# Joins of the stages in a two-layer transformer behind a causal attention, on one core

## The chip, the cores and the metric

The kernel runs on one core of one Trainium2 chip. The metric is the device time of one execution in microseconds, median of several runs. TensorE is PE in the profile, VectorE DVE, ScalarE ACT, GpSimd POOL, SyncE SP; SPq is the queue in which SP issues its DMAs, in order.

## The reference, cut to what matters

The input is x of 16 batches x 512 rows x 128 columns. A first part normalises the rows and computes causal attention; its result is added to the result of a two-layer transformer over the same normalised rows at the end. All is in float32. Here `shift_token` gives each row the second half of the row before it; that is what the "shifted rows" below are.

```python
def shift_token(t):
    t1, t2 = jnp.split(t, 2, axis=-1)
    t2 = jnp.pad(t2, ((0, 0), (1, 0), (0, 0)))[:, :-1]
    return jnp.concatenate([t1, t2], axis=-1)

def _layer(x, wqkv, qs, ksc, wo, lg, lb, w1, b1, w2, b2):
    h = shift_token(x)
    q, k, v = jnp.split(h @ wqkv, 3, axis=-1)        # 8 heads of 64
    q = l2norm(q) * qs
    k = l2norm(k) * ksc
    q, k = rotary_xpos(q, k)
    x = x + local_attention(q, k, v) @ wo            # window 64 and the one before
    h = shift_token(x)
    h = layernorm(h) * lg + lb
    a, g = jnp.split(h @ w1 + b1, 2, axis=-1)
    return x + (a * gelu(g)) @ w2 + b2
...
```

The first part is `softmax((q k^T + causal + bias) / 64) v` over 16 heads, times Wo, plus bo.

## The kernel before

There are five pieces of work, and each is a block: a block ends when all engines have done their part of it, and only then the next begins.

- `causal_attention` (L107) works through 16 batches of 8 slots, a slot being a pair of heads. SP loads the batches and stores the results (`turn`, L234); POOL scales the probabilities (L301). The normalised rows stay in the buffer `xf`, and the results are stored to `out` batch by batch.
- A block in `transformer` (L1329; the block is L1376 to L1424) prepares the rest: SP loads the rope table, the weights of layer 0 and the shifted rows of batch 0 into `hs`, and reads the 4 MB of `out` back into `acc` (L1386). DVE clears buffers, and POOL builds the masks.
- `local_attention` (L755) goes through 64 tiles of 128 rows, one per slot, with a pipeline five slots deep (`tile_slots`, L687; slot (b, t) is tile t of batch b, and (16, 0) is the last of the slots that drain it). DVE first splits the weights in a high and a low part (L930, L932), and POOL multiplies the tables (L817). In each slot SP issues the shifted rows of the tile (`load_shifted`, L719: two or three DMAs), and copies of `v` to other partitions (L799, L801) once ACT has written `v`. PE transposes the shifted rows (L1139) and multiplies them by the weights (L1040 to L1042). DVE adds the result to `xf` and counts `x_out` (L1011). Behind all slots SP loads the shifted rows of the gated stage's batches 0 and 1 into `hs2`.
- `gated_mlp` (L1145) goes through 16 batches of 512 rows, one per slot, four slots deep (`batch_slots`, L706). In slot b, SP loads the shifted rows of batch b with three DMAs once batch b-2 is normalised (`load_shifted_batch`, L731, DMAs at L735 to L737). DVE normalises batch b-1 (L1236), gates a third of batch b-2 (L1248), makes the statistics of batch b (L1255 to L1262), which wait for its rows, adds the result of batch b-3 to `xf` and counts `x_out` (L1266), and then gates the rest of b-2. POOL takes the power for the scale (L1196) and the low part of the transposed rows (L1192), and splits `w1` at the start (L1182, L1184). SP loads the next layer's attention weights at the start of the stage, and the shifted rows of the next attention stage's batch 0 at its end.
- The last block (L1430) adds `xf` to `acc` on DVE in four pieces (L1436), and SP stores each.

The two layers are a loop of the device, `nc.Fori(0, DEPTH)` (L1426); slots are unrolled. The order of the instructions of each engine is as written, and semaphores are the only other tie. The three DMAs of a gated batch:

```python
    sp.dma_start(hs[:, r, :, 0:half], x_b[:, :, 0:half]).then_inc(s_hs, 16)
    sp.dma_start(hs[1:P, r, :, half:D], x_b[0:P - 1, :, half:D]).then_inc(s_hs, 16)
    sp.dma_start(hs[0:1, r, 1:TT, half:D], x_b[P - 1:P, 0:TT - 1, half:D]).then_inc(s_hs, 16)
```

Of the kernel before, what the change touches and what calls it, by code (L numbers as in the profile page):

```python
# [12 lines left out]
P = 128  # L13
# [93 lines left out]
def causal_attention(nc, c, x, Wq, Wk, Wv, Wo, bo, rel, out, ext_dram):  # L107

    xf, ident, bank = c["xf"], c["ident"], c["bank"]
    with ExitStack() as ctx:  # L110
# [8 lines left out]
        wk_hi, wk_lo = sb("wk_hi", [P, HD], F32R), sb("wk_lo", [P, HD], F32R)  # L119
        wv_hi, wv_lo = sb("wv_hi", [P, HD], F32R), sb("wv_lo", [P, HD], F32R)  # L120
        wo = sb("wo_pairs", [P, HP, D])
        bo_b = sb("bo_b", [P, D])
        bias_tab = sb("bias_tab", [P, H, T])
# [89 lines left out]
        def _(sp):  # L213
# [31 lines left out]
            for half in range(2):  # L245
                sp.wait_ge(s_out[half], 16 * B)

        @block.gpsimd
        def _(pool):
# [39 lines left out]
            def slot(b, p, par):  # L289
# [455 lines left out]
def load_attention_weights(eng, c, d, l, s):  # L745

    def row(a):
        return a[bass.ds(l, 1), :].to_broadcast([P, DH])
    eng.dma_start(c["wqkv"][:], d["wqkv"][bass.ds(l, 1), :, :].squeeze(0)).then_inc(s, 16)
    eng.dma_start(c["wo4"][:], d["wo"][bass.ds(l, 1), :, :].squeeze(0).rearrange("(c p) n -> p c n", p=P)).then_inc(s, 16)  # L750
    eng.dma_start(c["qk_scale"][:, 0, :], row(d["q_scale"])).then_inc(s, 16)
    eng.dma_start(c["qk_scale"][:, 1, :], row(d["k_scale"])).then_inc(s, 16)


def local_attention(nc, c, d, l, w):  # L755
# [17 lines left out]
    def _(sp):  # L773

        s = sem["weights"]
        sp.dma_start(c["w1"][:], d["w1"][bass.ds(l, 1), :, :].squeeze(0)).then_inc(s, 16)
        sp.dma_start(c["w2"][:, 0:2, :], d["w2"][bass.ds(l, 1), 0:2 * P, :].squeeze(0).rearrange("(c p) n -> p c n", p=P)).then_inc(s, 16)
        sp.dma_start(c["w2"][0:CH[2], 2, :], d["w2"][bass.ds(l, 1), 2 * P:HID, :].squeeze(0)).then_inc(s, 16)
        sp.dma_start(c["w2"][CH[2]:CH[2] + 1, 2, :], d["b2"][bass.ds(l, 1), :]).then_inc(s, 16)
        with nc.allow_non_contiguous_dma(reason="a few columns, once a layer"):  # L780
            sp.dma_start(c["ln"][:, 0:1], d["ln_g"][bass.ds(l, 1), :].rearrange("l p -> p l")).then_inc(s, 16)
            sp.dma_start(c["ln"][:, 1:2], d["ln_b"][bass.ds(l, 1), :].rearrange("l p -> p l")).then_inc(s, 16)
            for part in range(2):
                for j in range(3):
                    o = part * HID + j * P
                    sp.dma_start(c["b1"][0:CH[j], part * 3 + j:part * 3 + j + 1],
                                 d["b1"][bass.ds(l, 1), o:o + CH[j]].rearrange("l p -> p l")).then_inc(s, 16)

        def slot(b, t):
            if not isinstance(b, int) or 0 < b < B:  # L790
# [4 lines left out]
            if two is not None:  # L795
# [16 lines left out]
    def _(pool):  # L812
        for n in w["mlp"].values():
            pool.sem_clear(n)

        for k in range(4):
            nc.gpsimd.tensor_tensor(tab[:, :, k, :], w["rope"][:, :, k, :],  # L817
                                    c["qk_scale"][:, k // 2, :].unsqueeze(1).to_broadcast([P, TT, DH]),
                                    ALU.mult).then_inc(sem["tab"], 1)
# [4 lines left out]
        def slot(b, t):  # L824
# [21 lines left out]
            if one is not None:  # L846
# [6 lines left out]
                nc.gpsimd.tensor_tensor(rn[:, r, :], ssq[:, r, :], w["mhalf"][:], ALU.pow).then_inc(sem["rn"], 1)  # L853
        tile_slots(pool, slot)

    @block.scalar
    def _(act):
        def slot(b, t):
# [21 lines left out]
            def rotated_out(k):  # L880
# [6 lines left out]
                dst = (qT[:], kT[:, :, WIN + ot * P:WIN + ot * P + P])[k]  # L887
# [613 lines left out]
```

## Time and profile before

| what | value |
|---|---|
| median of 3 runs | 2810.12 us (2809.82 to 2812.38) |
| the profiled execution, own time | 2812.22 us |
| its span, first to last instruction | 2810.4 us |
| mean granted clock of PE | 0.980 |
| busy: PE, DVE, ACT, POOL | 94%, 76%, 75%, 58% |
| first stage ends, attention of layer 0 begins | near 1422 us, first transpose at 1443 us |
| gated stage of layer 0 | 1969 to 2113 us |
| attention stage of layer 1 | 2117 to 2647 us |
| gated stage of layer 1 | 2647 to 2791 us |

The busy shares are averages over stages with different limits, so each stage is to be read by itself. Times in rows are microseconds from the span's start. In a timeline, the bracket at the end of a row gives how long the engine was idle before, and what ended it.

### The profile page before, as it was taken

Reading aid. Unit: us, or ns where it says so; the run is one execution under the profiler, and the core shown is the slowest. Engines: PE = TensorE matmul, PEld = TensorE weight load, DVE = VectorE, ACT = ScalarE, POOL = GpSimd, SP = SyncE. Lnnn points to the kernel's source line nnn. Section 1 sums busy time; section 2 is a strip of 40 time slices with the busy share of each in tenths; the row PEclk is TensorE's granted clock in tenths of the full one; section 3 lists DMA queues with packets and bytes.
Section 4 is the critical chain, followed back from the end, with each engine's and each line's share of the span. In section 5 each row is a group of like instructions: output and inputs, shape, how many; then the busy total and the mean of one; then the engine's idle time right before and its main releaser. Section 6 shows DMA issues by size and latency. Waiting matters only on the chain. (4 is left out here: it accounts for less than half of the span.)

```text
span 2810.4 us, 71245 instructions
## 1 busy us (share of the span) xinstructions
PE 2649.9 (94%) x24208; PEld 1999.9 (71%) x24208; DVE 2130.8 (76%) x5775; ACT 2099.4 (75%) x6207; POOL 1629.5 (58%) x1947
## 2 busy tenths in 40 slices
PE   7999999999999999999959999999797999999796
PEld 4666666666666666666638888887675888888575
DVE  5677777677776777767749999998567999999665
ACT  6777777777777777777729999999346999999642
POOL 4343434343444444334349999998226999999521
PEclk9999999999999999999979999999998999999898
DMA  2000000000000000000041111111111111111112
GB/s 70 7 7 9 9 5 7 7 9 9 5 9 5 9 9 5 9 5 5 5 112 39 40 40 40 39 39 38 45 29 35 40 39 41 40 41 39 45 34 77
DMA packets 128513, 77.07 MB, mean 27 GB/s; under 512 B 80196, under 2 KB 110736, under 8 KB 128144
## 3 DMA queue, kind: packets, MB, share of 16 engines
q1 hardware_dynamic: 127968, 72.34, 10.4%
q8 instruction: 199, 3.26, 0.5%
q14 instruction: 170, 1.39, 0.2%
q10 hardware_dynamic: 176, 0.07, 0.0%
HBM read 17.58 MB, written 8.41 MB: 9 GB/s over the span
## 5 line engine op out<-in xcount | busy, mean ns | idle before, releaser
L301 POOL TENSOR_SCALAR L<-L,rinv 128x128 f32<-128x128 f32 (+3 forms) x1024 | 522.7, 532 | 701.1 <-DVE rinv L482 701.1
L364 ACT ACTIVATE L<-L,nmax 128x128 f32<-128x128 f32 (+3 forms) x1024 | 565.1, 556 | 10.0 <-DVE nmax L469 1.2
L469 DVE CUSTOM_DVE_ANT_0 L<-bank,bias_tab 128x128 f32<-128x128 f32 (+3 forms) x1024 | 473.7, 486 | 95.9 <-PE bank L584 89.8
L876 ACT ACTIVATE f_L<-bank,f_nmax,f_rn 128x128 f32<-128x128 f32 x1024 | 459.8, 485 | 6.0 <-DVE f_nmax L1003 6.0
L853 POOL TENSOR_TENSOR f_rn<-f_ssq,f_mhalf 128x16 f32<-128x16 f32 x128 | 419.0, 3273 | 18.2 <-DVE f_ssq L987 4.6
L835 POOL TENSOR_TENSOR f_qkr<-f_ab 128x256 f32<-128x256 f32 x512 | 414.2, 837 | 11.3 <-DVE f_ab L954 11.3
L954 DVE TENSOR_TENSOR f_ab<-bank,f_tab 128x512 f32<-128x512 f32 x512 | 348.1, 680 | 8.3 <-ACT f_sq L866 8.3
L605 PE MATMUL bank<-ident,L 128*128 128x128 f32 x2560 | 351.0, 276 | 1.0 <-DVE PT L210 1.0
L605 PEld LDWEIGHTS bank<-ident,L 128*128 128x128 f32 x2560 | 289.3, 141 | 40.2 <-DVE PT L210 6.7
L210 DVE COPY PT<-bank 128x512 f32<-128x512 f32 x384 | 264.8, 690 | 51.9 <-PE bank L605 50.8
L623 PE MATMUL bank<-PT,v 128*64 128x512 f32 (+3 forms) x2048 | 303.9, 439 | 0.0
L210 ACT ACTIVATE PT<-bank 128x512 f32<-128x512 f32 x256 | 151.8, 593 | 168.0 <-PE bank L605 168.0
L623 PEld LDWEIGHTS bank<-PT,v 128*64 128x64 f32 x2048 | 126.8, 136 | 164.6 <-issue 129.5
L876 ACT ACTIVATION_READ_ACCUMULATOR f_L<-bank,f_nmax,f_rn 128x1 f32 x1024 | 239.4, 234 | 0.0
L332 ACT ACTIVATE k_hi<-bank 128x512 fp32r<-128x512 f32 x128 | 76.4, 597 | 206.2 <-PE bank L524 206.2
L1040 PE MATMUL bank<-f_w_hi,f_hT_hi 128*128 128x512 f32 x384 | 187.7, 489 | 12.0 <-DVE f_hT_lo L1016 11.5
L364 ACT ACTIVATION_READ_ACCUMULATOR L<-L,nmax 128x1 f32 x1024 | 197.6, 193 | 0.0
L584 PE MATMUL bank<-k_hi,q_hi 64*128 64x128 f32 (+3 forms) x1024 | 191.8, 371 | 0.7 <-ACT v L340 0.7
L978 DVE TENSOR_REDUCE f_rmax<-bank 128x4 f32<-128x512 f32 x256 | 164.9, 686 | 31.9 <-PE bank L1073 31.9
L866 ACT ACTIVATE f_sq<-bank 128x512 f32<-128x512 f32 x256 | 174.5, 682 | 13.0 <-PE bank L1042 13.0
L968 DVE TENSOR_REDUCE f_ssum<-f_sq 128x8 f32<-128x512 f32 x256 | 169.7, 663 | 0.0
L584 PE MATMUL bank<-k_lo,q_hi 64*128 64x128 f32 (+3 forms) x1024 | 165.6, 320 | 0.0
(145 smaller groups left out, 6409.6 us busy)
## 6 DMA issues: line engine op xcount, KB each, us to landing
f_vm<-f_v SPq DMA_DIRECT2D x224, 128.0 KB, 2.4
f_hs<-xf SPq DMA_DIRECT2D x132, 32.0 KB
f_hs<-xf SPq DMA_DIRECT2D x132, 31.8 KB
xb<-in_L_attn_x SPq DMA_DIRECT2D x16, 256.0 KB, 2.9
out<-yacc SPq DMA_DIRECT2D x32, 128.0 KB, 1.8
f_hs<-xf SPq DMA_DIRECT2D x32, 128.0 KB
out<-f_acc SPq DMA_DIRECT2D x4, 1024.0 KB, 7.5
f_hs<-xf SPq DMA_DIRECT2D x32, 127.0 KB
```

What stands on the lines that cost most here:

```text
L210: copy(PT[:, k, 0:n], ps_t[(h + k) % 2][:, 0:n], *how).then_inc(s_C[engine], 1)
L301: nc.gpsimd.tensor_scalar(t, t, rinv[:, h % RING, a, i:i + 1], 1.0, ALU.mult, ALU.mult).then_inc(s_N, 1)
L364: nc.scalar.activation(t, t, ACT.Exp, bias=nmax[:, p % RING, a, i:i + 1], scale=-1.0, accum_out=rsum[:, p % RING, a, i:i + 1]).then_inc(s_ ...
L469: nc.vector.tensor_tensor_reduce(out=L[:, p % RING, a, LOFF[i]:LOFF[i] + (i + 1) * P], in0=ps_s[a][i % 2][:, 0:(i + 1) * P], in1=bias_tab[ ...
L584: last[a] = nc.tensor.matmul(ps_s[a][i % 2][:, keys], qq[row, r, tok], kk[row, r, keys], start=(n == 0), stop=(n == 2))
L605: last = nc.tensor.transpose(ps_t[(h + k) % 2][:, n * P:n * P + P], L[:, h % RING, a, LOFF[i] + j * P:LOFF[i] + j * P + P], ident[:])
L623: last = nc.tensor.matmul(ps_o[DH * a:DH * a + DH, j * P:T], v[:, j, head:head + DH], PT[:, fill, off:off + T - j * P], start=(j == 0), st ...
L835: nc.gpsimd.tensor_tensor(halves(qkr[:, tt % 2, k], s), halves(ab[:, tt % 2, k, 0], s), halves(ab[:, tt % 2, k, 1], 1 - s), ALU.add).then_inc(
L853: nc.gpsimd.tensor_tensor(rn[:, r, :], ssq[:, r, :], w["mhalf"][:], ALU.pow).then_inc(sem["rn"], 1)
L876: nc.scalar.activation(L[:, ot % 2, a, k, :], ps_s[a][:, k * P:k * P + P], ACT.Exp, bias=nmax[:, ot % 2, a, k:k + 1], scale=rn[:, ot % 2, ...
L954: ins = nc.vector.tensor_tensor(ab[:, it % 2, k, n, :].rearrange("p (h e) -> p h e", h=FH), src[:].rearrange("p (h e) -> p h e", h=FH), ta ...
L1040: nc.tensor.matmul(ps[:], hT_hi[:, it % 2, :], w_hi[:, col], start=True, stop=False)
```

## The change

The loop over the layers is unrolled, and work is moved across the borders of the blocks. Masks and clearing of `hs` go to POOL in slot (0, 6) of the first stage; the shifted rows of batch 0 are loaded in its batch 1, and the weights of layer 0 in its batch 15, into parts of the buffer of the bias table; POOL multiplies tables and splits weights in the last slots (eight pieces). The attention stage loads the shifted rows of the gated batches 0 and 1 in slots (4, 0) and (5, 0), reads `out` back in slot (6, 0) of layer 0, and makes statistics and scale of batch 0 in its draining slots. The gated stage of layer 0 loads the next attention's shifted rows in slot 5 and lets POOL prepare that stage in slots 5 to 12. The gated stage of the last layer adds `xf` to `acc` on POOL per batch, adds the product to `acc` instead of `xf`, and stores each batch.

```diff
             def turn(b, par):
+                if b == B - 1:
+                    sp.wait_ge(s_L, at(b, 8 * HP, 8 * 4))
+                    load_attention_weights(sp, c, d, w, 0, w["s_load"])
+                if b == 1:
+                    sp.wait_ge(s_xf, 1)
+                    sp.wait_ge(w["s_hs_zero"], 1)
+                    for t in range(TT):
+                        load_shifted(sp, c["hs"], xf, 0, t, w["attn"][f"hs{t}"])
...
+                if (b, p) == (0, 6):
+                    build_masks(nc, pool, c, w)
+                for n in {(B - 1, 6): (0, 1, 2), (B - 1, 7): (3, 4, 5), (B, 0): (6, 7)}.get((b, p), ()):
+                    if n == 4:
+                        pool.wait_ge(s_V, HP * B)
+                    if n == 6:
+                        pool.wait_ge(s_k, HP * B)
+                    prepare_attention(nc, pool, c, w, n, w["s_load"])
...
+def prepare_attention(nc, pool, c, w, n, s_loaded):
+    sem, tab = w["attn"], w["tab"]
+    if n == 0:
+        pool.wait_ge(s_loaded, 16 * 5)
+    if n < 4:
+        nc.gpsimd.tensor_tensor(tab[:, :, n, :], tab[:, :, n, :],
+                                c["qk_scale"][:, n // 2, :].unsqueeze(1).to_broadcast([P, TT, DH]),
+                                ALU.mult).then_inc(sem["tab"], 1)
+    else:
+        some, t = ((0, 2), (2, 3))[(n - 4) // 2], w["w_two"][(n - 4) // 2]
+        raw = w["w_raw"][:, some[0] * FI:some[1] * FI]
+        if n % 2 == 0:
+            nc.gpsimd.tensor_copy(t[0], raw).then_inc(sem["w_hi"], 1)
+        else:
+            pool.wait_ge(sem["w_hi"], (n - 3) // 2)
+            nc.gpsimd.tensor_tensor(t[1], raw, t[0].bitcast(F32), ALU.subtract).then_inc(sem["w_lo"], 1)
...
 # local_attention, SP
+            if b in (4, 5) and t == 0:
+                sp.wait_ge(w["s_fill"], 4)
+                sp.wait_ge(sem["x_out"], 2 * TT)
+                load_shifted_batch(sp, w["hs2"], xf, b - 4, b - 4, w["mlp"][f"hs{b - 4}"])
+            if (l, b, t) == (0, 6, 0):
+                sp.dma_start(w["acc"][:], d["out"].rearrange("b (t p) d -> p (b t) d", p=P)).then_inc(w["s_acc"], 16)
         tile_slots(sp, slot, lag=2)
-        sp.wait_ge(sem["x_out"], 2 * TT)
-        for b in range(2):
-            load_shifted_batch(sp, w["hs2"], xf, b, b, w["mlp"][f"hs{b}"])
...
 # local_attention, POOL
-        for k in range(4):
-            nc.gpsimd.tensor_tensor(tab[:, :, k, :], w["rope"][:, :, k, :],
...
+        else:
+            nc.gpsimd.memset(kT[:, :, 0:WIN], 0.0).then_inc(w["s_fill"], 1)
+            nc.gpsimd.memset(vm[0:WIN, 0, :], 0.0).then_inc(w["s_fill"], 1)
+            nc.gpsimd.memset(w["hs2"][:], 0.0).then_inc(w["s_fill"], 1)
+            nc.gpsimd.memset(w["Hh"][:, :, 2, :], 1.0).then_inc(w["s_fill"], 1)
...
+            if (b, t) == (B, 2):
+                pool.wait_ge(sem["weights"], 16 * 12)
+                nc.gpsimd.tensor_copy(w["w1_hi"][:], c["w1"][:]).then_inc(w["mlp"]["w_hi"], 1)
...
+            if (b, t) == (B, 3):
+                batch_scale(nc, pool, w, 0)
...
 # local_attention, DVE
-        nc.vector.tensor_copy(w_hi[:], c["wqkv"][:]).then_inc(sem["w_hi"], 1)
-        dve.wait_ge(sem["w_hi"], 1)
-        nc.vector.tensor_tensor(w_lo[:], c["wqkv"][:], w_hi[:].bitcast(F32), ALU.subtract).then_inc(sem["w_lo"], 1)
         dve.wait_ge(sem["tab"], 4)
...
+            if (b, t) == (B, 2):
+                batch_statistics(nc, dve, w, 0)
+            if (b, t) == (B + 1, 0):
+                batch_normalise(nc, dve, w, 0)
+                batch_statistics(nc, dve, w, 1)
...
 # gated_mlp, SP
+        last = l == DEPTH - 1
+        if not last:
+            load_attention_weights(sp, c, d, w, l + 1, sem["weights"])
...
+            if 2 <= b < B:
+                sp.wait_ge(sem["hn"], at(b, TT, -TT))
+                load_shifted_batch(sp, hs, xf, b, r, sem[f"hs{r}"])
+            if not last and b == 5:
+                sp.wait_ge(sem["x_out"], 1)
+                for t in range(TT):
+                    load_shifted(sp, c["hs"], xf, 0, t, w["attn"][f"hs{t}"])
+            three = batch_back(b, 3)
+            if last and three is not None:
+                sp.wait_ge(sem["x_out"], three + 1)
+                sp.dma_start(ov[:, three * TT:three * TT + TT, :],
+                             w["acc"][:, three * TT:three * TT + TT, :]).then_inc(w["s_stored"], 16)
+        batch_slots(sp, slot, 3)
...
 # gated_mlp, POOL
+            if now is not None and b > 0:
+                batch_scale(nc, pool, w, b)
+            if l < DEPTH - 1 and 5 <= b < 13:
+                prepare_attention(nc, pool, c, w, b - 5, sem["weights"])
+            if l == DEPTH - 1 and now is not None:
+                pool.wait_ge(w["s_acc"], 16)
+                a = w["acc"][:, b * TT:b * TT + TT, :]
+                nc.gpsimd.tensor_tensor(a, a, xf[:, b * TT:b * TT + TT, :], ALU.add).then_inc(sem["acc"], 1)
...
 # transformer
-        with nc.Fori(0, DEPTH) as l:
+        for l in range(DEPTH):
             local_attention(nc, c, d, l, w)
             gated_mlp(nc, c, d, l, w)
-        with nc.Block() as block:
...
```

`batch_statistics`, `batch_scale` and `batch_normalise` hold the statements that the gated stage had for one batch, and `build_masks` those of the block that is gone. `load_attention_weights` issues five DMAs now, the rope table being the fifth, and loads into parts of one buffer.

## Rows read from the trace of the kernel before

**Rows 1.** Busy time by windows: us, then PE, PEld, DVE, ACT, POOL busy, clock, DMA.

```profile
1500.00:1900.00 400.00, 400.00 (x5103) 333.68 (x5103) 381.50 (x818) 392.82 (x1280) 385.83 (x307) 1.00 0.17 40
...
1990.00:2100.00 110.00, 102.64 (x631) 84.88 (x632) 68.03 (x228) 47.28 (x68) 30.68 (x28) 1.00 0.15 33
```

**Rows 2.** Waits of the whole span: total us, times, longest.

```profile
DVE f_stats L1255 <- DMA f_hs<-xf: 77.7, 28, 3.4
...
SPq L735 <- DVE f_hn L1236: 12.0, 2, 6.0
```

**Rows 3.** Timeline of SP and DVE, steady gated batches, layer 0: start, us, what.

```profile
2041.44 0.66 SPq L735 DMA_DIRECT2D f_hs<-xf  x1
...
2049.47 0.66 SPq L735 DMA_DIRECT2D f_hs<-xf  x1
...
2051.63 0.87 DVE L1255 BATCH_NORM_STATS2 f_stats<-f_hs 128x6 f32<-128x128 f32 x4 [2.82 <-DMA f_hs<-xf]
...
2053.16 0.69 DVE L1266 TENSOR_TENSOR xf<-bank,xf 128x512 f32<-128x512 f32 x1
```

**Rows 4.** Timeline, attention stage to gated stage of layer 1.

```profile
2646.80 0.29 DVE L1011 TENSOR_TENSOR xf<-bank,xf 128x128 f32<-128x128 f32 x1 [3.62 <-PE bank L1127]
...
2647.70 0.36 SPq L749 DMA_DIRECT2D f_wqkv<-in_L_ffn_wqkv  x1
...
2654.51 1.11 DVE L1236 TENSOR_SCALAR f_hn<-f_hs,f_mv,f_rstd 128x128 f32<-128x128 f32 x4 [5.45 <-POOL f_rstd L1196]
...
2655.65 0.66 SPq L735 DMA_DIRECT2D f_hs<-xf  x1
...
2657.00 0.17 DVE L1262 TENSOR_SCALAR f_ve<-f_mv 128x4 f32<-128x4 f32 x1
...
2665.89 0.88 DVE L1255 BATCH_NORM_STATS2 f_stats<-f_hs 128x6 f32<-128x128 f32 x4 [2.35 <-DMA f_hs<-xf]
```

**Rows 5.** Busy time by windows, one microsecond inside a gated batch of layer 0.

```profile
2055.50:2056.50 1.00, 1.00 (x11) 1.00 (x11) 1.00 (x4) 0.00 (x0) 0.00 (x0) 1.00 0.08 18
```

**Rows 6.** Timeline, first stage to attention stage of layer 0.

```profile
1422.80 0.11 POOL L1401 MEMSET f_mhalf<- 128x16 f32 x1 [13.45 <-POOLq L110]
...
1443.24 0.47 PE L1139 MATMUL bank<-ident,f_hs 128*128 128x128 f32 x1 [23.22 <-DVE f_w_lo L932]
...
1446.19 0.79 PE L1040 MATMUL bank<-f_w_hi,f_hT_hi 128*128 128x512 f32 x1 [2.47 <-DVE f_hT_lo L1016]
```

**Rows 7.** Groups by line: busy us, mean ns of one, idle before.

```profile
L283 POOL TENSOR_TENSOR wv_lo<-L,wv_hi 128x1024 fp32r<-128x1024 f32 x1 | 2.4, 2366 | 0.1
```

**Rows 8.** Timeline, POOL in the last slots of the first stage.

```profile
1405.28 4.08 POOL L301 TENSOR_SCALAR L<-L,rinv 128x128 f32<-128x128 f32 x8 [4.70 <-DVE rinv L482]
```

**Rows 9.** DMA issues: count, KB each, median us from issue to landing.

```profile
out<-yacc SPq DMA_DIRECT2D x32, 128.0 KB, 1.8
...
f_acc<-out SPq DMA_DIRECT2D x1, 0.5 KB, 18.7
```

**Rows 10.** Timeline, steady slots of the attention stage of layer 0.

```profile
1605.34 0.50 SPq L799 DMA_DIRECT2D f_vm<-f_v  x1
...
1616.03 0.27 PE L1139 MATMUL bank<-ident,f_hs 128*128 128x128 f32 x1
```

**Rows 11.** Timeline, end of layer 0's gated stage and start of layer 1.

```profile
2089.95 0.55 SPq L724 DMA_DIRECT2D f_hs<-xf  x1
...
2097.46 0.86 SPq L728 DMA_DIRECT2D f_hs<-xf  x1
...
2112.54 0.69 DVE L1266 TENSOR_TENSOR xf<-bank,xf 128x512 f32<-128x512 f32 x1 [3.04 <-PE bank L1292]
...
2120.40 0.48 PE L1139 MATMUL bank<-ident,f_hs 128*128 128x128 f32 x1 [7.90 <-DVE f_w_lo L932]
```

**Rows 12.** Timeline, the last sum of the last gated batch.

```profile
2790.27 0.69 DVE L1266 TENSOR_TENSOR xf<-bank,xf 128x512 f32<-128x512 f32 x1 [3.04 <-PE bank L1292]
```

**Rows 13.** Busy time by windows, start of layer 1's gated stage; clock is third from last.

```profile
2659.70:2664.50 4.80, 4.71 (x13) 3.86 (x14) 1.86 (x5) 1.61 (x3) 0.95 (x1) 0.50 0.08 20
```

More of the change, by code:

```diff
@@ new lines, in batch_statistics @@
+def batch_statistics(nc, dve, w, b):
+    sem, hs, stats, mv, ve = w["mlp"], w["hs2"], w["stats"], w["mv"], w["ve"]
+    dve.wait_ge(sem[f"hs{b % 2}"], 48 * (b // 2 + 1))
+    for t in range(TT):
+        nc.vector.bn_stats(stats[:, t, :], hs[:, b % 2, t, :]).then_inc(sem["stats"], 1)
+    dve.wait_ge(sem["stats"], at(b, TT, TT))
+    dve.wait_ge(sem["hn"], at(b, TT, 0))
+    dve.sem_inc(w["gate_dve"], 1)
+    for t in range(TT):
+        nc.vector.bn_aggr(mv[:, t, :], stats[:, t, :]).then_inc(sem["mv"], 1)
+    dve.wait_ge(sem["mv"], at(b, TT, TT))
+    nc.vector.tensor_scalar(ve[:], mv[:, :, 1], LN_EPS, None, ALU.add).then_inc(sem["ve"], 1)
@@ new lines, in batch_scale, with batch_normalise @@
+def batch_scale(nc, pool, w, b):
+    pool.wait_ge(w["mlp"]["ve"], b + 1)
+    nc.gpsimd.tensor_tensor(w["rstd"][:], w["ve"][:], w["mhalf"][:, 0:TT], ALU.pow).then_inc(w["mlp"]["rstd"], 1)
+def batch_normalise(nc, dve, w, b):
+    sem = w["mlp"]
+    dve.wait_ge(sem["rstd"], b + 1)
+    dve.wait_ge(sem["T_done"], b)
+    for t in range(TT):
+        nc.vector.tensor_scalar(w["hn"][:, t, :], w["hs2"][:, b % 2, t, :], w["mv"][:, t, 0:1], w["rstd"][:, t:t + 1],
+                                ALU.subtract, ALU.mult).then_inc(sem["hn"], 1)
@@ L1225, in _ @@
     def _(dve):
-        def gate():
-            dve.sem_inc(w["gate_dve"], 1)
         def slot(b, r):
             now, one, two, three = (batch_back(b, k) for k in range(4))
-            if one is not None:
-                dve.wait_ge(sem["rstd"], at(one, 1, 1))
-                dve.wait_ge(sem["T_done"], at(one, 1, 0))
-                for t in range(TT):
-                    nc.vector.tensor_scalar(hn[:, t, :], hs[:, 1 - r, t, :], mv[:, t, 0:1], rstd[:, t:t + 1],
-                                            ALU.subtract, ALU.mult).then_inc(sem["hn"], 1)
+            if one is not None and one > 0:
+                batch_normalise(nc, dve, w, one)
             def gated(j):
@@ L1426, in transformer @@
-        with nc.Fori(0, DEPTH) as l:
+        for l in range(DEPTH):
             local_attention(nc, c, d, l, w)
             gated_mlp(nc, c, d, l, w)
-        with nc.Block() as block:
-            @block.vector
-            def _(dve):
-                dve.wait_ge(s_acc, 16)
-                for q in range(4):
-                    a = acc[:, 16 * q:16 * q + 16, :]
-                    nc.vector.tensor_tensor(a, a, c["xf"][:, 16 * q:16 * q + 16, :], ALU.add).then_inc(s_sum, 1)
-            @block.sync
-            def _(sp):
-                ov = d["out"].rearrange("b (t p) d -> p (b t) d", p=P)
-                for q in range(4):
-                    sp.wait_ge(s_sum, q + 1)
-                    sp.dma_start(ov[:, 16 * q:16 * q + 16, :], acc[:, 16 * q:16 * q + 16, :]).then_inc(s_st, 16)
-                sp.wait_ge(s_st, 64)
@@ L1471, in program @@
              "w1": w1, "b1": b1, "w2": w2, "b2": b2, "rope": rope, "out": out}
-        causal_attention(nc, c, x, Wq, Wk, Wv, Wo, bo, rel, out, ext_dram)
-        transformer(nc, c, d)
+        w = {}
+        transformer_start(nc, ctx, c, w)
+        causal_attention(nc, c, d, w, x, Wq, Wk, Wv, Wo, bo, rel, out, ext_dram)
+        transformer(nc, c, d, w)
 _INS = ["L0_attn_x", "L0_attn_Wq", "L0_attn_Wk", "L0_attn_Wv", "L0_attn_Wo", "L0_attn_bo", "L0_attn_rel_pos_bias",
```

228 lines of the change are left out of this document (102 added, 126 removed).

## The prediction

> **What bounds the kernel now.** I read first which engine is full in which stage (busy time by windows), then who waits for whom, then the timelines around the five joins and one steady batch of each later stage. Shares are of one stage each. In a windowed-attention stage ACT is busy 392.8 of 400 us, POOL 385.8, and PE without a gap [rows 1]: nothing there absorbs a delay. In the gated stage PE is busy 102.6 of 110 us, 7.5 of each 8.03, and DVE only 68.0 [rows 1]. What sets the pace there is neither: DVE waits 28 times for the shifted rows, 77.7 us in all, while the SP queue waited only twice for the statement that frees the buffer [rows 2]. SP issues these loads back to back: L735 at 2041.44 and again at 2049.47, so a batch takes 8.03 us [rows 3]. From L735 to the statistics that use the batch pass 2051.63 - 2041.44 = 10.2 us [rows 3]; a load that found the queue empty took as long, 2665.89 - 2655.65 = 10.2 us [rows 4]. While such a load runs, the 16 DMA engines are 0.08 busy at 18 GB/s [rows 5], little more than one engine of 16, so one 256-byte run takes 256 B / 18 GB/s = 14.2 ns, and the 127 x 4 = 508 runs of L736 some 7.2 us.
>
> The Trainium skill says why, on the page DMA: Bandwidth & Descriptors (Why a DMA increments its semaphore by 16 and not by 1): a transfer is split over the largest number of engines, at most 16, that divides its slowest dimension, which for 127 partitions is one. It speaks against this change, which moves such transfers into busier places; the rows above give the same price without it.
>
> **The change, part by part.** Negative is a gain.
>
> (a) First join. Before, the last stage's stores end and the next block's first instruction is at 1422.80, but the first transpose comes at 1443.24, after the loads, the weight split and the tables, and the first product 2.95 us later [rows 6]. With all of that done earlier, the transpose starts about 0.1 us into the block: -20.3, and 1 us more (0 to 2) as the chain to the product no longer waits for the tables: **-21.3**. The cover of what moves: POOL gets eight pieces, none over the 2.37 us of the 128x1024 subtraction [rows 7]; POOL idles 4.70 us before its scaling in a last slot [rows 8], and gets 3 + 3 pieces of about 1 us, one of them 2.4, per slot. The masks and the zeroing go into slot (0, 6) in the same way. I price both at 0; without the cover the nine microseconds of POOL would show. The 11 shifted loads go past SP in batch 1, the five weight loads in batch 15; SP has only one load and two stores per batch of that stage, each waiting for its data, so 0. Clearing `hs2`, `Hh`, `kT` and `vm` on POOL at the block's start is done before its first rotation: 0 to +1.
>
> (b) Read-back of the first stage's result, 4 MB, moved from before the block to tile slot (6, 0) of layer 0. It takes 18.7 us to land [rows 9]. Behind it in the same queue stand the shifted rows of tile (6, 1). In a steady slot SP is free for them when `v` is out, at 1605.34, and PE wants them at 1616.03, 10.7 us later [rows 10]. The read-back is issued 1.15 us into that time (two `vm` copies, the first 0.50), lands at 1.15 + 18.7 = 19.9, and the 127 runs behind it need 1.8 more: 21.7 - 10.7 = **+11.0** (0, if it is passed by, to +14).
>
> (c) The shifted rows of gated batches 0 and 1 are issued in slots (4, 0) and (5, 0) of each layer instead of after the stage. Same queue, same reasoning: 1.15 + 10.2 + 1.8 = 13.2 against 10.7 us, +2.5 each, four times: **+10.0** (0 to +13). Slots have no slack [rows 1].
>
> (d) Join into the gated stage. The last residual sum ends at 2647.09, and 2655.65 is the first shifted load, which waited for the normalised batch 0 [rows 4]. After: that batch's normalisation and the statistics of batch 1 stand behind the last residual sum on DVE (slot (16, 0) adds the sum first); the same two pieces took 2654.51 to 2657.17, 2.7 us. Then the block changes in 0.6 us (2647.09 to 2647.70 [rows 4]), so SP is there at 2650.4. Since loads set the pace, only their start counts: 2655.65 - 2650.4 = **-5.3** in layer 1. In layer 0 SP issues five weight loads first, now with the rope table among them, and their bytes run ahead of L736 on every engine: **0** (-5 to +1). POOL's split of `w1`, in the drain of the attention stage, 0.
>
> (e) Gated stage of layer 0: the 11 shifted loads for the next attention stage move from behind the last batch to slot 5. They took 2089.95 to 2098.32 in the queue [rows 11], hidden by the last three slots. Now load 6 stands behind them, and the queue is the bound: **+8.4** (+4 to +9). POOL's eight preparations fall into its idle time: 0.
>
> (f) Join gated to attention: the last sum ends at 2113.2, the first transpose is at 2120.40 [rows 11]. After: 2113.8, so -6.6, and a little of the chain behind it: **-7.0**.
>
> (g) Gated stage of layer 1. SP now does, in slot b: load batch b, **wait for x_out of batch b-3**, store batch b-3. Queued behind this wait is the load of batch b+1. DVE makes x_out(b-3) in slot b after the statistics of b, which wait for load b itself. So load b+1, issued before at the end of load b, now starts after: statistics to end of x_out, 2053.16 + 0.69 - 2051.63 = 2.2 us; two hand-overs, 0.1; the store's issue, taken as 0.66 like L735, which has as many runs; then 10.2 until the statistics of b+1 [rows 3]. 2.2 + 0.1 + 0.7 + 10.2 = 13.2 us instead of 8.03. Loads 4 to 15 stand behind a store: 12 x 5.17 = **+62.0** (12 x 4.6 to 12 x 5.7). POOL's sum per batch is beside it: 0.
>
> (h) End. Before, the last sum ends at 2790.96 and the span at 2810.4, 19.4 us for four large sums and 4 MB of stores [rows 12]. After: one 256 KB store, between the 1.8 us of a 128 KB one [rows 9] and 3.5; I take 2.8: **-16.6**.
>
> Sum: -21.3 + 11.0 + 10.0 + 0 - 5.3 + 8.4 - 7.0 + 62.0 - 16.6 = +41.2 us. The profiled execution took 2812.22 us (span 2810.4), 2.1 above the median of the runs; so 2853.4 against it, and 2810.12 + 41.2 = **2851** for the median.
>
> **The rivals.**
> A, the other side: the new wait costs nothing, because a load that starts on an empty queue lands sooner. It decides from 13.2 - 8.03 = 5.2 us less, a landing within 5.0 us of its issue. Then +62.0 is gone: 2789 us, faster. For it: the 10.2 us of a steady load include the draining of the one before. Against it: the first load of layer 1 had an empty queue and took 10.2 too [rows 4].
> The Trainium skill has on the same page (Anatomy of one DMA) a fit of 2.0 us plus bytes over 436 GB/s; by it the 256 KB land in 2.6 us, and with (b), (c) and (e) shrunk likewise the time would be near 2764. It was fitted for another issuing path, and rows 3 and 4 show 10.2.
> B: PE at its lower level. At 13.2 us per batch PE is busy 7.5 / 13.2 = 57%. Over 4.8 us behind the waits of the second join into the gated stage it was granted 0.50 of its clock, the 1.2 of its two levels of 1.2 and 2.4 GHz [rows 13]. If it stays there, 15.0 us of work exceed 13.2: +1.8 x 12 = 22, so 2873. Against it: 5 us at half speed and the rest at full still make 10 us, which fit.
> C: the loads of (b) and (c) don't hold the attention stage, -21: 2830. For it: PE's order might leave a slack that one slot doesn't show.
> D: the change doesn't shorten the first join as it says, since POOL's late pieces wait for the weight loads: some +10, 2861.
>
> **How the numbers follow.** Forecast 0.68, A 0.08, B 0.08, C 0.14, D 0.02. The bound between faster, same and slower is 0.2% (5.6 us), about what a measurement of this kernel can tell from no change. All but A are slower. Of A, 0.06 are faster, 0.02 within the bound, where the landing is shorter by half. The forecast's own range is 2831 to 2865, from (g) +-7, (b), (c), (e) and the joins some +-10 together. Taking in C and most of B gives 2822 to 2875, which leaves out A and the tails.
>
> **What would show it.** In the profile after: statistics of the last gated stage some 13 us apart, and SP waiting for DVE's x_out before each store; PE busy under 60% there. In the attention stage of layer 0 one gap of about 11 us before a transpose at slot (6, 1), and in each layer two of 2 to 3 us. One gap of 8 us more between two statistics in the first gated stage. The first transpose of layer 0 within 1 us of its block's start, and the end 3 us after the last sum. I am wrong if the last gated stage keeps 8 us per batch.

## The result, and the profile after

The changed kernel takes 2868.1 us (median of 4 runs, 2864.51 to 2873.1), the kernel before 2810.13: a ratio of 1.021 with a 95% interval of 1.0197 to 1.0223. The profiled executions are 2867.04 and 2812.22 us, 54.8 apart. So it is slower, 17 us above the forecast of 2851 and 3 above the forecast's own range of 2831 to 2865; the wider range of 2822 to 2875 holds it.

The page of the kernel after, busy time and 40 slices of its span:

```profile
span 2865.2 us, 71094 instructions
...
PE 2690.6 (94%) x24208; PEld 2035.3 (71%) x24208; DVE 2128.0 (74%) x5764; ACT 2101.8 (73%) x6206; POOL 1660.7 (58%) x1974
...
PE   7999999999999999999899899997889999999677
...
PEclk9999999999999999999999999998999999999878
```

The last slices are where PE thins out and its clock sinks. The waits of the kernel after over the whole span (total us, times, longest), to hold against [rows 2]:

```profile
DVE f_stats L826 <- DMA f_hs<-xf: 141.8, 28, 11.5
...
SPq L1288 <- DVE f_acc L1373: 77.1, 16, 7.9
...
PE bank L1250 <- DMA f_hs<-xf: 21.2, 5, 9.5
```

DVE's wait for shifted rows grew from 77.7 to 141.8 us, SP waits for a sum before each store of the last gated stage, where it waited for none before, and PE waits for shifted rows in the attention stages, five times. One batch of the last stage, to hold against [rows 3] (timeline of SP and DVE):

```profile
2697.31 0.87 DVE L826 BATCH_NORM_STATS2 f_stats<-f_hs 128x6 f32<-128x128 f32 x4 [7.43 <-DMA f_hs<-xf]
...
2698.85 0.69 DVE L1373 TENSOR_TENSOR f_acc<-bank,f_acc 128x512 f32<-128x512 f32 x1
...
2699.57 0.38 SPq L1288 DMA_DIRECT2D out<-f_acc  x1
...
2700.00 0.66 SPq L754 DMA_DIRECT2D f_hs<-xf  x1
2700.70 0.71 SPq L755 DMA_DIRECT2D f_hs<-xf  x1
2701.45 6.54 SPq L756 DMA_DIRECT2D f_hs<-xf  x1
...
2710.08 0.87 DVE L826 BATCH_NORM_STATS2 f_stats<-f_hs 128x6 f32<-128x128 f32 x4 [7.29 <-DMA f_hs<-xf]
```

That is the loop of step (g), link by link: statistics, sum (1.5 us later), store, load, and 10.1 us from the load's first issue to the next statistics. The period is 12.8 us. Over twelve such batches, by windows (us, then PE, PEld, DVE, ACT, POOL busy, granted clock, DMA share, GB/s):

```profile
2684.39:2838.50 154.11, 114.88 (x566) 97.63 (x564) 63.06 (x204) 43.82 (x63) 42.94 (x37) 0.83 0.17 41
```

PE is busy 75% of this stretch, 9.6 us per batch, and not under 60% as forecast: at a mean granted clock of 0.83 the 7.5 us of work take longer.

Where the time went, by the start of the same instruction in both traces (us). "Tile" is the transpose of the shifted rows of a tile in an attention stage, counted from 0 in each layer; "batch" the statistics of a gated batch.

```
landmark                           before    after     difference
layer 0  tile 0                    1443.24   1424.61   -18.6
         tile 16                                       -21.0
         tile 24, behind two early loads               -11.3
         tile 26, behind the read-back                         +0.7
         tile 63                   1937.19   1938.57    +1.4
         batch 2                   1987.38   1990.99    +3.6
         end of the last sum       2113.23   2124.99   +11.8
layer 1  tile 0                    2120.40   2125.46    +5.1
         tile 4                                         +1.0
         tile 16                                        +1.2
         tile 24, behind the early loads               +11.7
         tile 63                   2614.35   2628.20   +13.9
         batch 2                   2665.89   2676.43   +10.5
         batch 15                  2769.76   2838.50   +68.7
         end of the last sum       2790.96   2862.52   +71.6
         end of the span           2810.4    2865.2    +54.8
```

The two largest entries between neighbours are the last gated stage, +58.2, and the first join, -21.0. The others show where the forecast's sizes were off. The timeline of PE in the attention stages of the kernel after:

```profile
1424.61 0.40 PE L1250 MATMUL bank<-ident,f_hs 128*128 128x128 f32 x1 [3.38 <-PEq L110]
...
1637.93 0.47 PE L1250 MATMUL bank<-ident,f_hs 128*128 128x128 f32 x1 [9.51 <-DMA f_hs<-xf]
...
2258.46 0.48 PE L1250 MATMUL bank<-ident,f_hs 128*128 128x128 f32 x1 [3.10 <-DMA f_hs<-xf]
```

The first stands 0.2 us behind the block's start. The second is slot (6, 1), behind the 4 MB, and the third is one of the four waits behind the early loads of a batch. The cost does not end with the wait, as the busy time by windows (granted clock third from last, then the DMA share and GB/s) shows, first during and after the wait of 9.51, then after that of 3.10:

```profile
1628.00:1637.00 9.00, 0.42 (x4) 0.18 (x2) 0.91 (x2) 0.85 (x4) 2.17 (x4) 0.77 0.92 250
1637.00:1643.00 6.00, 5.07 (x42) 4.24 (x43) 3.32 (x8) 2.74 (x11) 2.48 (x2) 0.50 0.15 35
```

```profile
2258.00:2267.00 9.00, 8.54 (x87) 6.97 (x88) 4.93 (x11) 5.44 (x16) 5.72 (x4) 0.65 0.10 23
```

### The profile page after: what moved, and what is told of

Read it like the earlier page. It is cut to its first block and busy times, and to the rows that moved or that the text cites. A ratio compares the mean times of both kernels' runs of the same rounds, so it can differ in the third digit from the quotient of the medians.

```text
span 2865.2 us, 71094 instructions
## 1 busy us (share of the span) xinstructions
PE 2690.6 (94%) x24208; PEld 2035.3 (71%) x24208; DVE 2128.0 (74%) x5764; ACT 2101.8 (73%) x6206; POOL 1660.7 (58%) x1974
## 3 DMA queue, kind: packets, MB, share of 16 engines
q1 hardware_dynamic: 126544, 71.49, 10.1%
## 5 line engine op out<-in xcount | busy, mean ns | idle before, releaser
L383 ACT ACTIVATE L<-L,nmax 128x128 f32<-128x128 f32 (+3 forms) x1024 | 564.9, 556 | 10.1 <-DVE nmax L488 1.4
L488 DVE CUSTOM_DVE_ANT_0 L<-bank,f_rows 128x128 f32<-128x128 f32 (+3 forms) x1024 | 473.5, 485 | 95.7 <-PE bank L603 90.1
L936 POOL TENSOR_TENSOR f_qkr<-f_rows 128x256 f32<-128x256 f32 x512 | 412.4, 835 | 25.1 <-DVE f_rows L1059 25.1
L1059 DVE TENSOR_TENSOR f_rows<-bank,f_rows 128x512 f32<-128x512 f32 x512 | 347.8, 680 | 15.1 <-ACT f_sq L975 15.1
L1399 PE MATMUL bank<-f_w,f_Hh 128*128 128x128 f32 (+1 forms) x768 | 120.7, 319 | 61.6 <-DVE f_Hh L1363 61.6
L945 POOL TENSOR_TENSOR f_L<-f_L,f_rinv 128x512 f32<-128x512 f32 x128 | 133.4, 1042 | 72.2 <-DVE f_rinv L1048 56.0
```

Of the source, the lines that this page charges most:

```text
L383: nc.scalar.activation(t, t, ACT.Exp, bias=nmax[:, p % RING, a, i:i + 1], scale=-1.0, accum_out=rsum[:, p % RING, a, i:i + 1]).then_inc(s_ ...
L488: nc.vector.tensor_tensor_reduce(out=L[:, p % RING, a, LOFF[i]:LOFF[i] + (i + 1) * P], in0=ps_s[a][i % 2][:, 0:(i + 1) * P], in1=bias_tab[ ...
L936: nc.gpsimd.tensor_tensor(halves(qkr[:, tt % 2, k], s), halves(ab[:, tt % 2, k, 0], s), halves(ab[:, tt % 2, k, 1], 1 - s), ALU.add).then_inc(
L1059: ins = nc.vector.tensor_tensor(ab[:, it % 2, k, n, :].rearrange("p (h e) -> p h e", h=FH), src[:].rearrange("p (h e) -> p h e", h=FH), ta ...
```

## The experiments

**1. The place of the store.** The new wait came with a new transfer. Which of them costs 5 us per batch? One kernel stores a batch one slot later and waits for a sum that is a slot older; the other keeps the wait in its place and stores everything at the end.

```diff
-            three = batch_back(b, 3)
+            four = batch_back(b, 4)
...
-        batch_slots(sp, slot, 3)
+        batch_slots(sp, slot, 4)
```

> The changed kernel, but in the last gated stage SP stores batch b-4 in slot b instead of b-3, so that the wait for x_out is over when SP comes to it; the bytes stored are the same. Theory W (order: the load of batch b+1 stands behind the wait for x_out of b-3): the statistics of that stage come every 8.0 to 8.5 us again instead of 12.84, SP shows no wait for x_out, and the time falls by 12 x 4.6 = 52 to 58 us, to 2810 to 2816 us, less the clock that PE gets back. Rival S (bytes: the 512-byte runs of the stores take the DMA engines from the shifted rows): the period stays above 11 us and the time above 2845.

Measured: 2810.69 us (10 runs), ratio to the kernel before 1.0001 (0.9991 to 1.001); 57.4 less than the change. Its timeline in the last stage:

```profile
2700.66 0.42 SPq L1288 DMA_DIRECT2D out<-f_acc  x1
2701.13 0.65 SPq L754 DMA_DIRECT2D f_hs<-xf  x1
...
2701.82 0.71 SPq L755 DMA_DIRECT2D f_hs<-xf  x1
...
2702.57 6.55 SPq L756 DMA_DIRECT2D f_hs<-xf  x1
2702.69 0.88 DVE L826 BATCH_NORM_STATS2 f_stats<-f_hs 128x6 f32<-128x128 f32 x4 [3.16 <-DMA f_hs<-xf]
...
2709.17 0.42 SPq L1288 DMA_DIRECT2D out<-f_acc  x1
```

The store is issued without a wait for the sum (that of this slot comes only at 2704.24), and SP's queue is full from end to end: 0.42 + 0.65 + 0.71 + 6.55 and the gaps are 8.5 us, the period. Nothing waits for a result any more; the queue itself is the bound.

```diff
                 sp.wait_ge(sem["x_out"], three + 1)
-                sp.dma_start(ov[:, three * TT:three * TT + TT, :],
-                             w["acc"][:, three * TT:three * TT + TT, :]).then_inc(w["s_stored"], 16)
         batch_slots(sp, slot, 3)
         if last:
+            for q in range(B):
+                sp.dma_start(ov[:, q * TT:q * TT + TT, :],
+                             w["acc"][:, q * TT:q * TT + TT, :]).then_inc(w["s_stored"], 16)
```

> The changed kernel with the same waits for x_out of batch b-3 in every slot, but no store between them: the sixteen stores follow at the end. Theory W: the period stays at 12.84 less the 0.43 us of the store's issue, 12.4 us. Rival S: with no stores in the stage the period falls to 8.0. Both: about 14 us more at the end for 4 MB of stores behind each other, against 2.7 now.

Measured: 2870.43 us (one run), no gain. The period of the last stage is (2830.82 - 2682.44) / 12 = 12.36 us with the wait alone (statistics of batches 15 and 3), against 12.84 with the store and 7.99 before. So 4.37 of the 4.85 us are the order, 0.5 the store's own place in the queue. In the first kernel the store stays and the period is 8.51, 0.5 above the kernel before. The late stores give the 0.5 back: the end is 37.8 us behind the statistics of batch 15 instead of 26.7.

**2. The read-back.** The same 4 MB in 16 pieces of a batch each, one per batch of layer 0's attention stage.

```diff
-            if (l, b, t) == (0, 6, 0):
-                sp.dma_start(w["acc"][:], d["out"].rearrange("b (t p) d -> p (b t) d", p=P)).then_inc(w["s_acc"], 16)
+            if l == 0 and b < B and t == 2:
+                sp.dma_start(w["acc"][:, b * TT:b * TT + TT, :],
+                             d["out"].rearrange("b (t p) d -> p (b t) d", p=P)[:, b * TT:b * TT + TT, :]).then_inc(w["s_acc"], 16)
...
-                pool.wait_ge(w["s_acc"], 16)
+                pool.wait_ge(w["s_acc"], 16 * B)
```

> The changed kernel, but the first stage's result is read back in 16 pieces of 256 KB, one per batch of layer 0's attention stage at tile 2, instead of 4 MB at slot (6, 0). Theory Q (queue: the shifted rows of tile (6, 1) stand behind 4 MB): PE's wait of 9.5 us before a transpose goes, each piece costs nothing (about 1.5 us of queue against 4 us of slack), and the stage shortens by 12 us: 2856 us. Rival R (the 4 MB cost what their bytes cost, wherever they go): the pieces give 16 stalls of 0.7 us, and the time stays near 2868.

Measured: 2850.16 us (4 runs), ratio to before 1.0143 (1.0126 to 1.016), 17.9 less than the change. The transpose of slot (6, 1) no longer waits:

```profile
1623.49 0.27 PE L1251 MATMUL bank<-ident,f_hs 128*128 128x128 f32 x1
```

This trace is 2.3 us ahead of the change's at its first tile, 4.8 at tile 24, 16.7 at tile 26 and 16.6 at tile 63: the place of the read-back is worth 11.9, as expected, and the pieces cost nothing that shows. The rest lies in places whose code is the same; experiment 3 shows one source of it.

**3. GpSimd beside DVE in the drain.** Both attention stages drained 3.5 and 2.4 us slower than before. There GpSimd now subtracts the halves of `w1`, at the same time as DVE's last scaling of the probabilities. The third kernel does it behind that scaling, and behind the batch's scale, which POOL took after it in the change.

```diff
-            if (b, t) == (B, 2):
+            if (b, t) == (B, 3):
+                batch_scale(nc, pool, w, 0)
+                pool.wait_ge(sem["probs_odd"], TT * B)
                 pool.wait_ge(sem["weights"], 16 * 12)
...
```

> The changed kernel, but POOL splits w1 one slot later in the drain of the attention stages, behind the last scaling of probabilities by DVE. Theory P (port: DVE's scaling, 2.12 us instead of 0.69, ran beside POOL's subtraction): it takes 0.7 us again, PE's wait of 2.5 us before the last transposes shrinks by 1.4, and each drain is 1.4 to 3.5 us shorter. Rival K (the drain is longer because PE was granted half its clock, whatever POOL does): DVE's scaling stays at 2.1 us or the drain stays as long.

Measured: 2853.99 us (one run), 14.1 less, twice what was expected. The scaling, in the change and then in this kernel (timeline of DVE):

```profile
1963.99 2.12 DVE L1097 TENSOR_TENSOR f_L<-f_L,f_rinv 128x512 f32<-128x512 f32 x1
```

```profile
1961.27 0.69 DVE L1097 TENSOR_TENSOR f_L<-f_L,f_rinv 128x512 f32<-128x512 f32 x1
```

The same instruction took three times as long beside GpSimd's. From tile 63 to batch 2 the stage is 3.7 us shorter in layer 0 and 3.6 in layer 1: 7.3 for the two drains, just above the expected 1.4 to 3.5 each. The slower scaling is the smaller part of it. From its start to PE's transposes pass 2.2 us in the change and 0.8 here, and from the transposes to the last residual sum 7.1 and 5.2, with the same 52 matmuls (change, then this kernel):

```profile
1966.16:1973.27 7.11, 5.78 (x52) 5.04 (x52) 0.29 (x1) 1.19 (x2) 0.84 (x1) 0.59 0.00 0
```

```profile
1962.02:1967.20 5.18, 3.86 (x52) 3.37 (x52) 0.29 (x1) 1.20 (x2) 2.41 (x3) 1.00 0.00 0
```

So PE waited 2.29 us for the scaling instead of 0.72, and behind that wait its clock fell. Rival K had the clock as the cause whatever POOL does; it is part of the cost here, but in this stretch it fell only behind the longer wait. The profiled executions are 13.0 apart. Of the other 5.7 us 4.0 came in layer 1 at tiles 17 to 22, whose code is the same: after the first early load the clock stayed up, where the change fell to 0.65 (above). The rest, 1.7, is spread and left open.

```profile
2252.40 0.33 PE L1250 MATMUL bank<-ident,f_hs 128*128 128x128 f32 x1 [2.70 <-DMA f_hs<-xf]
```

```profile
2252.00:2261.00 9.00, 8.60 (x121) 7.23 (x122) 7.37 (x16) 8.01 (x27) 6.16 (x5) 1.00 0.20 46
```

A PE wait of 2.70 us with no drop, one of 3.10 with a drop: a short stall's cost depends on whether the clock falls, and that differs between executions of the same instructions.

**4. The split of the 127 partitions.** In the costly places but two (the read-back and `w1`) the same thing stood behind the wait: a load of some 10 us whose last issue blocks SP for 6.5. Is this the count of 127? The shifted half is loaded in two pieces of 112 and 15 partitions, nothing else, first in the kernel before, then in the change. The loader of single tiles is split in the same way, and the semaphore counts follow (48 becomes 64).

```diff
-    sp.dma_start(hs[1:P, r, :, half:D], x_b[0:P - 1, :, half:D]).then_inc(s_hs, 16)
+    sp.dma_start(hs[1:113, r, :, half:D], x_b[0:112, :, half:D]).then_inc(s_hs, 16)
+    sp.dma_start(hs[113:P, r, :, half:D], x_b[112:P - 1, :, half:D]).then_inc(s_hs, 16)
```

> The kernel before, with the shifted half of the rows (127 partitions, 1 to 127) loaded in two pieces, of 112 and of 15 partitions, in both loaders; nothing else. Theory E (the piece of 127 partitions is carried out badly and blocks SP's queue behind it: in the gated stages of before SP's three issues of a batch take 0.66 + 0.70 + 6.54 us with gaps of some 0.05, which is the whole period of 8.03): the blocked issue falls to about 0.7, from the first issue of a batch to its landing it is under 6 us instead of 10.2, DVE's wait for f_hs in the gated stages goes, and the period falls to what TensorE needs, its busy 37.65 us of 40 = about 7.55 us. With 28 batches x 0.4 = -11, and up to -10 at the joins, where the transposes wait for the first rows: 2787 to 2800 us. Rival F (the time is that of the 256-byte pieces or of the queue, whatever the partitions): the load is as long, with one issue of 0.7 more in a batch: the period is 8.7, 28 x 0.7 = +20, 2830 us.

> The changed kernel with the same split, nothing else; the store stays where it is. Theory E: from the sum of batch b-3 to the landing of batch b it is then 0.4 (store issued) + 4 x 0.7 (issues) + about 2 instead of 11.2, so the wait of SP costs little or nothing: the period of layer 1's gated stage falls from 12.84 to under 8.3 us (-54 or more), the eleven shifted rows of slot 5 of layer 0 from +8.7 to about +1, the four stalls of the attention tiles behind the rows of batches 0 and 1 (+20 measured) to under +4, and the gated batches gain what they gain in the kernel before split (about 0.4 each): 2868 - 54 - 8 - 16 - 11 = 2779 us, 2765 to 2795. Rival F: nothing of it falls, and each batch has an issue more: 2875 to 2895.

Measured, on the same chip: the kernel before with the split 2786.09 us (ratio 0.9919, 0.9902 to 0.9935), the change with the split **2752.83** (ratio to before 0.9797, 0.9781 to 0.9813). Four issues in the split kernel of before, and a window of its gated stage, then the last stage of the changed one:

```profile
2043.51 0.68 SPq L736 DMA_DIRECT2D f_hs<-xf  x1
2044.23 0.65 SPq L737 DMA_DIRECT2D f_hs<-xf  x1
2044.92 0.91 SPq L738 DMA_DIRECT2D f_hs<-xf  x1
2045.87 0.73 SPq L739 DMA_DIRECT2D f_hs<-xf  x1
```

```profile
2030.00:2070.00 40.00, 40.00 (x254) 34.47 (x253) 28.22 (x94) 19.67 (x28) 13.01 (x12) 1.00 0.19 40
```

```profile
2655.66 0.38 SPq L1290 DMA_DIRECT2D out<-f_acc  x1
2656.09 0.68 SPq L755 DMA_DIRECT2D f_hs<-xf  x1
2656.81 0.65 SPq L756 DMA_DIRECT2D f_hs<-xf  x1
2657.51 0.91 SPq L757 DMA_DIRECT2D f_hs<-xf  x1
2658.46 0.73 SPq L758 DMA_DIRECT2D f_hs<-xf  x1
...
2660.72 0.87 DVE L828 BATCH_NORM_STATS2 f_stats<-f_hs 128x6 f32<-128x128 f32 x4 [0.48 <-DMA f_hs<-xf]
```

The block is gone (0.73 instead of 6.54), PE has no gap in 40 us, and the period is 7.29 us instead of 8.03: the gated stages were bound by a queue, and are bound by PE now. In the change a load is in place 4.6 us after its first issue instead of 10.1, so the wait for the sum still stands in SP's queue and costs nothing: the last stage has 7.3 us per batch there too. Step by step, the change with the split is ahead of the change by 9.7 us in the first attention stage (no wait behind the early loads), 21.2 in the first gated stage, 9.7 in the second attention stage and 71.9 from there to the end. In the attention stages only the read-back still stops PE, for 9.9 us. The gain is larger than expected: 2752.83 lies 12 below the expected 2765 to 2795. Of the 71.9 us from the second attention stage to the end, 67.1 are twelve periods of 7.25 instead of 12.84, for which 54 or more had been expected.

**5. Is it the divisor?** Two other splits of the 127 in the kernel before, 61 and 66, and 106 and 21.

> The kernel before with the 127 rows split as 61 and 66 instead of 112 and 15. Theory E1 (the number of engines that carry a piece is the largest one up to 16 that divides its count of partitions: 127 and 61 give one, 66 gives 11, 112 gives 16): the issue behind the piece of 61 is held in proportion to what one engine has to carry, at most 6.54 x 61/127 = 3.1 us, at least 1.5; the period of the gated stages is still TensorE's 7.29 us, the time about that of the split of 112 and 15, 2782 to 2792 us. Rival E2 (only the total matters, any split into two takes the block away): every issue of a batch takes under 1 us, as with 112 and 15.

> The kernel before with the split 106 and 21 (106 is 2 x 53, 21 is 3 x 7). Theory E1: 106 partitions go over two engines, 53 each, so the issue behind is held at most 6.54 x 53/127 = 2.7 us, at least 1.2. Rival E3 (a count that 16 does not divide goes to one engine, whatever its divisors): held 6.54 x 106/127 = 5.5 us. By both the time stays near 2790 us, since the hold is then no longer than TensorE's batch; what tells is the length of the issues.

Measured: 2787.32 and 2785.52 us, one run each. SP's timeline, first 61 and 66, then 106 and 21; L737 issues the first piece, L738 the second:

```profile
2042.89 0.72 SPq L737 DMA_DIRECT2D f_hs<-xf  x1
2043.65 2.61 SPq L738 DMA_DIRECT2D f_hs<-xf  x1
2046.32 0.72 SPq L739 DMA_DIRECT2D f_hs<-xf  x1
```

```profile
2046.77 0.72 SPq L737 DMA_DIRECT2D f_hs<-xf  x1
2047.54 2.22 SPq L738 DMA_DIRECT2D f_hs<-xf  x1
2049.81 0.71 SPq L739 DMA_DIRECT2D f_hs<-xf  x1
```

The issue behind the piece is held 6.54 us for 127 partitions, 2.61 for 61, 2.22 for 106 and 0.91 for 112. E2 (any split frees the queue) fails at 2.61, E3 (all that 16 does not divide goes to one engine) at 2.22, for which it wanted 5.5. If 127, 61 and 106 / 2 = 53 partitions are what one engine carries, the holds lie near one line: (6.54 - 2.61) / 66 = 0.060 us per partition, (2.61 - 2.22) / 8 = 0.049. That is 14.9 ns for a 256-byte run by the longer stretch; from 18 GB/s it was 14.2.

The Trainium skill's rule (DMA: Bandwidth & Descriptors, Why a DMA increments its semaphore by 16 and not by 1) gives just these counts: the largest number up to 16 that divides the partitions, 1 for 127 and 61, 2 for 106, 16 for 112. The traces agree with it in these four holds; they show no engine by itself. The time does not tell the splits apart: 2786.09, 2787.32 and 2785.52 us, with 7.3 us per gated batch in all three, since even a hold of 2.61 leaves the queue shorter than PE's work.

**6. What can be had.** The read-back in pieces and `w1` behind the scaling, with the split (store as in the change, then one slot later), and without the split (store late).

> The changed kernel with the split, the read-back of the output in 16 pieces (one per batch of layer 0's attention stage) and w1's halves on GpSimd behind the last scaling of the probabilities; the store stays where the change has it, one batch behind the third. Theory E: the read-back costs -12 to -16 less than in the run with the split alone, w1 -7 less: 2768 minus 20 = about 2750 us, 2740 to 2775, below the kernel before and below the split of before. Rival F: about 2860.

> As the run before it in this list, and the store one slot later (behind the sum of batch b-4). Theory E with the load short: the place of the store no longer matters, so the same as with the store in its place, within 3 us. If the wait of SP still costs something with the short load (the landing is then later than TensorE's need by some tenths of a us), this one is 5 to 15 us faster. Rival F: about 2800 (the late store's gain stays, the split costs 20).

> The changed kernel with the store one slot later, the read-back in 16 pieces and w1 behind the scaling, but without the split: what can be had if the loads stay as they are. The three effects add if they lie at different places: 2868.1 - 57.4 (late store) - 18 (read-back) - 7 (w1, drain of two stages; its one look was at -14, of which 7 lay outside the drains) = 2786 us, 2775 to 2796. If they do not add (the piece by piece read-back and the late store share SP's queue only in different stages, so I see no way), 2800 or more.

Measured: 2737.18 us (ratio 0.9743, 0.9727 to 0.9759) with the store in its place, 2738.1 (0.974, 0.9724 to 0.9757) with the store late: with a short load its place does not matter. The first is a little under its expected 2740 to 2775, the second within the expected 3 us of the first. The gain on the split alone is 15.7 us by the medians, 18.0 by the profiled executions; of those 12.6 lie in layer 0's attention stage and 5.4 between the attention stages' ends and the gated stages' (1.9 and 3.5). Without the split 2792.93 (0.9938, 0.9923 to 0.9954): the sum of the single gains, expected at 2786, held within 7.

The last kernel adds one thing: the shifted rows for the next attention stage are issued in four slots, one tile each, instead of all in slot 5.

```diff
-            if not last and b == 5:
+            if not last and 5 <= b < 5 + TT:
                 sp.wait_ge(sem["x_out"], 1)
-                for t in range(TT):
-                    load_shifted(sp, c["hs"], xf, 0, t, w["attn"][f"hs{t}"])
+                load_shifted(sp, c["hs"], xf, 0, b - 5, w["attn"][f"hs{b - 5}"])
```

> As the run with split, read-back in 16 pieces and w1 later, and the shifted rows of batch 0 for the attention stage, eleven (with the split fifteen) issues in one slot of layer 0's gated stage, one tile in each of four slots. There the statistics waited 3.66 us for a load; DVE's period was 11.02 in that slot, 5.14 in the next, against 7.29. Theory S (SP's queue of fifteen issues is what is left there): -2 to -4, 2734 us. Rival N (TensorE hid it, the next periods of 5.14 took it back): within 1 us of 2737.

Measured: 2735.42 us, ratio 0.9731 (0.9718 to 0.9744), not told apart from the 0.9743 without it. The statistics around those slots are 7.27 us apart, where one gap of 11.01 had stood. The medians differ by 1.8 us, the profiled executions by 0.1. This trace is 2.4 us behind the other at tile 63 of layer 0, before the edit acts, and level with it at the fifth tile of layer 1: 2.4 us gained in between, which is what theory S wanted (2 to 4). But first tiles scatter by as much from trace to trace, the whole gain is not told apart from none, and neither S nor rival N (PE's order hides the gap) is shown.

## Why the prediction was right, and where its sizes were off

The sign, the mechanism and the place of the main term were right, and 2868.1 lies in the range of 2822 to 2875, though 3 us above the forecast's own 2831 to 2865. By its own steps, forecast and measured:

- **(a) first join**, -21.3: -21.0, in other parts than forecast. The first stage's last sum came 1.2 us later (1421.27 for 1420.06), an offset that is there from that stage's first sum on, so it does not come from POOL's late pieces. Counted from that sum, the join gave -22.2: -19.8 at the first transpose (forecast -20.3), and 2.4 more by tile 16, where the forecast had 1. That the number fits within 0.3 is partly luck.
- **(b) read-back**, +11.0: +12.0. The wait lasted 9.51; behind it PE worked at 0.50, its 1.2 of 1.2 and 2.4 GHz, for the 6 us of the window above, and the next tile lost 2.3.
- **(c) early loads**, +10.0: +9.7 in layer 0 and +10.5 in layer 1, so **+20.2**. This is the mis-sized term: twice its forecast, and 7 above its own bound of 13. The four jumps of the tiles that waited are 3.65, 2.78, 3.28 and 2.72, 12.4 together. But the tiles behind lost 1.6, 1.5, 2.7 and 1.7 more, with a granted clock of 0.81, 0.81, 0.67 and 0.82 over the 9 us behind the four waits. In the traces of experiments 2 and 3 the clock stayed at 1.00 behind both loads of layer 1, and there the two cost 6.6 us together instead of 10.5. So the wait alone is some 3.3 us each for the forecast 2.5, and the rest is the clock. The step took a stall in a stage without slack for the length of the wait alone.
- **(d) join into the gated stage**, -5.3 and 0: -3.4 in layer 1 and +2.2 in layer 0, both with the drain in them. It had priced POOL's split of `w1` in the drain at 0. Experiment 3 puts 3.6 to 3.7 us per layer on it: the cover was there on POOL, but the cost arose on DVE (1.4 us of slower scaling in layer 0) and then on PE (1.9 at the lower clock behind it).
- **(e) eleven loads in slot 5**, +8.4: +8.7, the two statistics around them 16.7 us apart instead of 8.0.
- **(f) join into the attention stage**, -7.0: -10.8, counted to the fifth tile: -6.7 at the first, as forecast, and -4.1 more while the pipeline fills, where the forecast had 0.4. That part was not broken down.
- **(g) the wait**, +62.0: +58.2, 12 periods of 12.84 instead of 7.99. The store's issue took 0.38, not 0.66. Experiment 1 shows that it is the wait's place, not the transfer.
- **(h) end**, -16.6: -16.8, but the last batches themselves drained 2.9 later.
- Not in the forecast: 3.1 us of small drifts in the attention stages, and -0.5 in the rest of layer 0's gated stage. Their cause is open. With them the terms give the +54.8 of the spans.

Rival A needed a landing within 5.0 us of the issue on an empty queue. The load took 10.1 again, so the new wait was fully paid. With the split it takes 4.6, and then A is what happens: the change becomes 33.3 us faster than the kernel before with the same split (2786.09 to 2752.83). Rival B did not come: PE is granted 0.55 while it waits with 2.10 us of work in 5.70, then 0.88 over the next 7 us in which it works without a gap, and all of it fits into the 12.8 us. C fell with the jumps of the tiles behind the early loads, D with the first transpose, 0.2 us behind its block's start. The kernel after, busy time by windows in the last stage:

```profile
2697.30:2703.00 5.70, 2.10 (x10) 2.10 (x11) 5.27 (x17) 0.00 (x0) 2.25 (x2) 0.55 0.28 71
2703.00:2710.00 7.00, 7.00 (x38) 5.89 (x37) 0.00 (x0) 3.23 (x5) 1.29 (x1) 0.88 0.07 17
```

The fit of 2.0 us plus bytes over 436 GB/s in the Trainium skill (DMA: Bandwidth & Descriptors, Anatomy of one DMA), made for another issuing path, gives 2.6 us, far below the 10.1 measured here. For the split load, 2660.72 - 2658.46 = 2.3 us pass from the issue of the last, small piece to the statistics, near its fixed part.

What I missed is not in a step but ahead of them. The prediction named one engine of 16 as the cause of the slow load and used it as a price. It did not ask what the kernel would be without it, which is worth more (-115 us on the change) than anything the change does.

## What to carry to other kernels

Where a wait for a result stands in an in-order DMA queue with the next load behind it, the period can't be shorter than the way to the result, the store's issue and the full landing time of that load, here 2.2 + 0.4 + 10.1 us; so shorten the landing first, then judge the order. The same change is 2.1% slower or 1.2% faster by that alone (2786.09 to 2752.83). A load that shifts rows by one partition is worth cutting in two; with 112 partitions, which 16 divides, in the large piece it held the queue least (0.91 us), though 61 and 106 gave the same time here. And a stall of some us in a stage where PE is full is to be priced at the wait plus the lower clock behind it, here 1.2 to 1.9 times the wait.

## What the runs showed of the hardware

- The issue that follows a piece of 127 partitions with four 256-byte runs each holds SP's queue for 6.54 us; behind 61, 106 and 112 partitions it is 2.61, 2.22 and 0.91. An issue that takes 6.5 us in SP's timeline is the sign.
- DVE's 128x512 multiply in SBUF took 2.12 us beside GpSimd's subtraction and 0.69 alone; GpSimd's own instruction took 1.62 us beside it and 1.63 alone.
- PE's granted clock went to 0.50 after a wait of 9.51 us. Behind the twelve waits of 2.5 to 3.5 us in the traces of the change and of experiments 2 and 3 it fell to 0.66 to 0.82 over 9 us seven times and stayed at 1.00 five times, with the same instructions. What decides it was not found.
- 256 KB in pieces of 128, 112 and 15 partitions are in place 4.6 us after the first of four issues, which themselves take 3.0.
